# Second expert stage: weighted rows added into the output by the scatters, instead of loads and sums at the end

## What is computed

```python
x = x + 0.5 * _L0_ffn_ref(_layernorm(x, axis=-1), router_w, gate_w, up_w, down_w)
x = x + _L0_attn_ref(_layernorm(x, axis=-1), W_qkv, W_out)
x = x + 0.5 * _L0_ffn_ref(_layernorm(x, axis=-1), router_w, gate_w, up_w, down_w)
```

```python
top_vals, top_idx = jax.lax.top_k(x @ router_w.T, 2)
routing_weights = jax.nn.softmax(top_vals, axis=-1)
combine = jnp.sum(jax.nn.one_hot(top_idx, E) * routing_weights[..., None], axis=1)
for e in range(E):
    y = (jax.nn.silu(x @ gate_w[e].T) * (x @ up_w[e].T)) @ down_w[e].T
    out = out + combine[:, e:e + 1] * y
```

## Time and profile before

| what | us |
| --- | --- |
| median of 3 runs | 1253.74 (1253.63 to 1253.86) |
| profiled execution | 1255.44 |
| its span, first to last instruction | 1253.70 |
| first expert stage, about | 0 to 260 |
| attention, about | 260 to 1016 |
| second expert stage, about | 1016 to 1253.7 |
| first and last start of a scatter in it (line 1250) | 1037.8, 1235.0 |

### The profile page before, as it was taken

The page is one execution under the profiler, slowest core; times in us unless marked ns, Lnnn a source line. Parts: engine busy times, 40 slices in busy tenths (PEclk is TensorE's granted clock), DMA queues, the critical chain, the costliest instruction groups (busy, mean ns, idle before and its releaser), DMA issues. The chain is left out here.

```text
span 1253.7 us, 28419 instructions
## 1 busy us (share of the span) xinstructions
PE 1195.8 (95%) x8838; PEld 911.9 (73%) x8838; DVE 904.5 (72%) x2002; ACT 791.6 (63%) x2272; POOL 810.7 (65%) x884
## 2 busy tenths in 40 slices
PE   7799999979999999999999999999999989999993
PEld 6588888856666666666666667766666668888883
DVE  6775344448888888888888998788998877733543
ACT  4665665646766676667666667766666665555553
POOL 4233356248878778778788787577566536666663
PEclk8899999989999999999999999999999989999997
DMA  9135222132222222222221222221221331113223
GB/s 323 31 97 153 60 55 71 44 72 46 54 60 54 46 56 54 58 46 51 60 57 41 57 60 60 60 52 36 51 52 40 97 116 43 45 48 114 62 65 116
DMA packets 81614, 86.54 MB, mean 69 GB/s; under 512 B 11248, under 2 KB 70512, under 8 KB 81088
## 3 DMA queue, kind: packets, MB, share of 16 engines
q1 hardware_dynamic: 70976, 64.98, 20.0%
q0 software_dynamic: 8864, 18.17, 5.6%
q10 hardware_dynamic: 1632, 1.57, 0.4%
HBM read 33.43 MB, written 17.69 MB: 41 GB/s over the span
## 5 line engine op out<-in xcount | busy, mean ns | idle before, releaser
L2003 POOL TENSOR_SCALAR at_prob<-at_prob,at_rec 128x128 f32<-128x128 f32 (+3 forms) x256 | 312.0, 1223 | 156.8 <-DVE at_rec L2214 154.8
L2401 ACT ACTIVATE at_prob<-at_s,at_nb 128x128 f32<-128x128 f32 (+3 forms) x512 | 264.7, 535 | 16.9 <-DVE at_nb L2206 13.6
L2412 ACT ACTIVATE at_probT<-at_pt 128x128 f32<-128x128 f32 (+3 forms) x256 | 105.2, 437 | 225.6 <-PE at_pt L2110 225.3
L2206 DVE TENSOR_REDUCE at_nb<-at_s 128x2 f32<-128x256 f32 (+3 forms) x256 | 203.2, 815 | 9.4 <-PE at_s L2096 9.4
L1564 DVE TENSOR_TENSOR f_hid<-f_b,f_silu 128x512 f32<-128x512 f32 x142 | 98.4, 693 | 135.8 <-PE f_b L1311 96.1
L2110 PE MATMUL at_pt<-ident,at_prob 128*128 128x128 f32 x1280 | 183.9, 276 | 5.2 <-DVE at_prob L2217 1.9
L2200 DVE TENSOR_TENSOR at_turned<-at_pj,rope 128x1024 f32<-128x1024 f32 x122 | 148.7, 1219 | 46.2 <-PE at_pj L2057 43.2
L2091 PE MATMUL at_s<-at_KT,at_QT 64*128 64x128 f32 (+3 forms) x1024 | 176.5, 463 | 4.9 <-DMA at_KT<-at_probT 2.7
L1997 POOL TENSOR_TENSOR at_R<-at_turned 128x512 f32<-128x512 f32 x126 | 157.5, 1270 | 24.1 <-DVE at_turned L2200 24.1
L2110 PEld LDWEIGHTS at_pt<-ident,at_prob 128*128 128x128 f32 x1280 | 141.7, 142 | 26.7 <-issue 14.6
L2121 PE MATMUL at_o<-at_probT,at_V 128*64 128x128 f32 (+2 forms) x1792 | 152.9, 322 | 0.0
(11 more groups left out here) (336 smaller groups left out, 2258.3 us busy)
## 6 DMA issues: line engine op xcount, KB each, us to landing
at_QT<-at_R SPq DMA_DIRECT2D x128, 128.0 KB, 2.4
at_KT<-at_R SPq DMA_DIRECT2D x124, 128.0 KB, 2.4
ys_dram<-y SPq DMA_DIRECT2D x71, 64.0 KB, 1.8
f_down<-down_t SPq DMA_DIRECT2D x2, 2048.0 KB, 7.6
f_xb<-xn_dram,f_source POOLq DMA_INDIRECT x142, 2.6
X<-x SPq DMA_DIRECT2D x4, 512.0 KB, 6.1
gate<-gate_t SPq DMA_DIRECT2D x8, 256.0 KB, 5.1
f_up<-up_t SPq DMA_DIRECT2D x8, 256.0 KB, 6.7
```

Source lines behind the costliest of these rows:

```text
L2003: pool.tensor_scalar(w, w, rec[:, q, 1:2], None, ALU.mult).then_inc(probB_ready, 1)
L2206: dve.tensor_reduce(nb[:, q, :], s_bank[q % 2][:, :, 0:(q + 1) * P], axis=AX, op=ALU.max, negate=True).then_inc(nb_ready, 1)
L2401: act.activation(prob[q][:, h, :], s_bank[q % 2][:, h, 0:n], ACT.Exp, bias=nb[:, q, h:h + 1], scale=1.0, accum_out=sums[:, q, h:h + 1]).th ...
L2412: act.activation(probT[0][:, 0:q + 1, q * P:(q + 1) * P], pt_bank[0][:, at:at + (q + 1) * P].rearrange("p (b r) -> p b r", r=P), ACT.Copy) ...
```

## The change

The second stage no longer brings rows back. Its scatters add each row straight into `out`, which holds X by then:

- The normed rows of the second stage are stored twice, in `xw_dram`, once for each of a token's two experts, with 129 columns. The 129th is the token's weight for that expert, stored apart by `store_shares` as single numbers, once for the leading half (in attention) and once for the rest (in the second stage).
- A gather brings 129 columns, so each row comes with its weight. There are seven tiles `xb` instead of four (`HELD`), since the weight is read later than the row. DVE multiplies the hidden product by it, in one `scalar_tensor_tensor` in the place of `tensor_tensor`.
- The scatter writes to `out` with `compute_op=ALU.add`. Scatter 0 waits until all of X is stored in `out`, and scatter j waits until scatter j-1 has landed. Rows without a token go to 128 further rows at the end of `out`, which the host cuts off. `targets` takes eight operations for its list in the place of six, `sources` two in the place of four.
- X is stored to `out` during attention, a group at a time (`FINISHED`), the last group at the start of the second stage. The late rows are stored after four blocks have been turned.
- The weights are made earlier: for the leading half in attention, for the rest in steps 6 (`odds`) and 9 (`shares`) of the second stage.
- All loads, sums and stores behind the last scatter and the sums between the steps are gone; the end waits for the last scatters.
- At the beginning of attention PE does 24 transposes whose result nobody reads (`WARM`), ahead of the wait for the first copies of QT and KT.

```diff
     def gather(...):
         if j in (0, sure):
-            pool.wait_ge(self.xn_out, 16 * (self.NB // 4 if j else self.LEAD // 4))
-        rows = self.NB * P if j >= sure else self.LEAD * P
+            pool.wait_ge(self.xn_out, 32 * (self.NB // 4 if j else self.LEAD // 4))
+            pool.wait_ge(self.shares_out, 64 if j else 32)
+        rows = 2 * (self.NB if j >= sure else self.LEAD) * P
         pool.indirect_dma_start(
-            out=self.xb[j % self.AHEAD][:, :], out_offset=None, in_=self.xn_dram[0:rows, :],
+            out=self.xb[j % self.HELD][:, :], out_offset=None, in_=self.xw_dram[0:rows, :],
...
     def store(self, sp, g, xn):
         sp.wait_ge(self.xn_ready, g + 1)
-        sp.dma_start(self.xn_dram[4 * g * P:4 * (g + 1) * P, :].rearrange("(n p) d -> p n d", p=P), xn[:, :, :]
-                     ).then_inc(self.xn_out, 16)
+        for k in range(2):
+            sp.dma_start(self.rows(g, k)[:, :, 0:P], xn).then_inc(self.xn_out, 16)
+
+    def store_shares(self, sp, r):
+        sp.wait_ge(self.shares_ready, r + 1)
+        tiles = self.routing.tiles[r]
+        for k in range(2):
+            sp.dma_start(self.rows(tiles.start // 4, k, len(tiles))[:, :, P:P + 1],
+                         self.routing.wts[:, 2 + k, tiles.start:tiles.stop].rearrange("p (n a) -> p n a", a=1),
+                         allow_slow_non_contiguous=True).then_inc(self.shares_out, 16)
...
     # second stage, SP
+                    g = GROUPS - 1
+                    sp.dma_start(out[4 * g * P:4 * (g + 1) * P, :].rearrange("(n p) d -> p n d", p=P),
+                                 X[:, 4 * g:4 * g + 4, :]).then_inc(stored, 16)
+                    sp.wait_ge(xt_psum, AHEAD)
                     for g in LATE_GROUPS:
                         sp.wait_ge(xn_ready, g + 1)
-                        sp.dma_start(xn_dram[4 * g * P:4 * (g + 1) * P, :].rearrange("(n p) d -> p n d", p=P),
-                                     late_xn[:, 4 * g - LEAD:4 * g + 4 - LEAD, :]).then_inc(xn_out, 16)
-                    scattered(sp)
-                    ...
-                    sp.wait_ge(stored, 16 * GROUPS)
+                        for k in range(2):
+                            sp.dma_start(lead.rows(g, k)[:, :, 0:P], late_xn[:, 4 * g - LEAD:4 * g + 4 - LEAD, :]
+                                         ).then_inc(xn_out, 16)
+                    lead.store_shares(sp, 1)
+                    for k in range(AHEAD):
+                        sp.wait_ge(y_out[k], 16 * ((BLOCKS - k + AHEAD - 1) // AHEAD))
...
     # second stage, POOL: scatter(j)
                     pool.wait_ge(routing.lists_ready, routing.TARGETS[j >= SURE])
                     pool.wait_ge(y_ready, j + 1)
+                    if j == 0:
+                        pool.wait_ge(stored, 16 * (GROUPS + 1))
+                    else:
+                        pool.wait_ge(y_out[(j - 1) % AHEAD], 16 * ((j - 1) // AHEAD) + 16)
                     pool.indirect_dma_start(
-                        out=ys_dram, out_offset=bass.IndirectOffsetOnAxis(ap=routing.target[:, j:j + 1], axis=0),
-                        in_=y[k][:, :], in_offset=None).then_inc(y_out[k], 16)
+                        out=out, out_offset=bass.IndirectOffsetOnAxis(ap=routing.target[:, j:j + 1], axis=0),
+                        in_=y[k][:, :], in_offset=None, compute_op=ALU.add).then_inc(y_out[k], 16)
...
     # second stage, ACT
                 for j in range(-1, BLOCKS + 3):
                     step(act, j, j % AHEAD)
+                    if lead and j == CHOOSE_AT + 2:
+                        routing.odds(act, 1, exp_ready)
...
     # second stage, DVE
-                        dve.tensor_tensor(hid[k][:, :], up_bank[k][:, :], silu[k][:, :],
-                                          ALU.mult).then_inc(hid_ready, 1)
+                        if lead:
+                            dve.scalar_tensor_tensor(out=hid[k][:, :], in0=up_bank[k][:, :],
+                                                     scalar=xb[j % len(xb)][:, P:P + 1], in1=silu[k][:, :],
+                                                     op0=ALU.mult, op1=ALU.mult).then_inc(hid_ready, 1)
...
     # attention, SP
+                sp.dma_start(out[NB * P:(NB + 1) * P, :], ident[:, :]).then_inc(lead.stored, 16)
                 for n in range(ROTATIONS):
...
+                    if n - EARLY in FINISHED:
+                        g = FINISHED[n - EARLY]
+                        sp.wait_ge(y_used, 8 * g + 8)
+                        sp.dma_start(out[4 * g * P:4 * (g + 1) * P, :].rearrange("(n p) d -> p n d", p=P),
+                                     X[:, 4 * g:4 * g + 4, :]).then_inc(lead.stored, 16)
...
+                lead.store_shares(sp, 0)
...
     # attention, PE
+                pe.wait_ge(rope_ready, 2)
+                for _ in range(WARM):
+                    pe.transpose(s_bank[0][:, 0, 0:P], ident[:, :], ident[:, :])
                 for i in range(STEPS + 2):
```

More of the change, by code:

```diff
@@ L413, in shares @@
             last.then_inc(done, 1)
-            dve.wait_ge(done, 1)
     def totals(self, dve, r, totals):
@@ L529, in blocked, with first_number @@
                           ALU.is_equal).then_inc(self.block_ready, 1)
+    def first_number(self, r, k):
+        if self.home is not None:
+            return k * self.NB + self.tiles[r].start
+        return 2 * self.tiles[r].start + k * self.n[r]
     def numbered(self, dve, r, k):
@@ L533, in numbered @@
         some = slice(k * n, (k + 1) * n)
-        first = k * self.NB + self.tiles[r].start
+        first = self.first_number(r, k)
         number = self.const.numbersb[:, first:first + n]
@@ L593, in sources @@
         blank, token, found = self.blank[:, some], self.token[:, some], self.found
+        if self.home is None:
+            link(dve.scalar_tensor_tensor(out=token, in0=found[:, 0, some], scalar=float(P), in1=found[:, 1, some],
+                                          op0=ALU.mult, op1=ALU.add))
+            dve.tensor_scalar(self.source[:, some], token, -1.0, 0.0, ALU.add, ALU.max).then_inc(self.lists_ready, 1)
+            return
         link(dve.tensor_scalar(blank, found[:, 0, some], float(self.NB), None, ALU.is_ge))
@@ L690, in __init__ @@
         self.routing.place_lists(room)
-        self.xb = [room(f"xb{k}", [P, P]) for k in range(self.AHEAD)]
+        self.xb = [room(f"xb{k}", [P, P + 1]) for k in range(self.HELD)]
+        self.exp_ready = sem("exp_ready")
+        self.shares_ready = sem("shares_ready")
+        self.shares_out = sem("shares_out")
         self.xb_in = [sem(f"xb_in{k}") for k in range(self.AHEAD)]
@@ L1277, in _ @@
                         scatter(j - 3)
-                if out is not None:
-                    for m, (g, tiles) in enumerate(((BY_POOL, slice(0, 4)), (SHARED, slice(2, 4)))):
-                        some = X[:, 4 * g + tiles.start:4 * g + tiles.stop, :]
-                        for k in range(2):
-                            pool.wait_ge(weighted, 2 * m + k + 1)
-                            if k:
-                                pool.wait_ge(pool_added, 2 * m + 1)
-                            pool.tensor_tensor(some, lead_got[g % LEAD_GROUPS][:, k, tiles, :], some, ALU.add
-                                               ).then_inc(pool_added, 1)
             @block.tensor
@@ L1555, in step @@
                     route_later(j)
-                    if out is not None and j in SUMMED:
-                        sum_leading(SUMMED[j])
                     if projection is not None and j in PREPARED_AT:
@@ L1606, in route_later @@
                         routing.pack(dve, 1)
[L1607 removed]
+                    if j == TAKE_AT + 5 and lead is None:
                         routing.shares(dve, 0, exp_ready)
[L1610 to L1620 removed]
+                    if j == CHOOSE_AT + 5 and lead:
+                        routing.shares(dve, 1, exp_ready, lead.shares_ready)
                 def prepare_first(m):
@@ L1684, in _ @@
                         trailing(SPLIT[j - 1])
-                if projection is None:
-                    routing.shares(dve, 1, exp_ready, shares_ready)
-                    added = 0
-                    for g, tiles in ((BY_DVE[0], range(0, 4)), (BY_DVE[1], range(0, 4)), (SHARED, range(0, 2))):
-                        dve.wait_ge(got_in[g % LEAD_GROUPS], 64)
-                        for k in range(2):
-                            if k:
-                                dve.wait_ge(dve_added, added)
-                            for t in tiles:
-                                n = 4 * g + t
-                                dve.scalar_tensor_tensor(out=X[:, n, :], in0=lead_got[g % LEAD_GROUPS][:, k, t, :],
-                                                         scalar=wts[:, 2 + k, n:n + 1], in1=X[:, n, :],
-                                                         op0=ALU.mult, op1=ALU.add).then_inc(dve_added, 1)
-                                added += 1
         work.close()
@@ L1905, in attention @@
         EARLY = 3
```

(2 more changed lines are left out.)

128 lines of the change are left out of this document (40 added, 88 removed).

## The result

The changed kernel takes 1346.0 us (median of 4 runs, 1345.08 to 1348.26) where the kernel before takes 1253.7 (1253.63 to 1253.86): 1.0732 times as long, with a 95% interval of 1.0718 to 1.0746. That is 92.3 us more; 38 were forecast. The profiled execution took 1348.26 us, its span 1346.5.

A forecast was written before the change was run, and what follows sets the result against it. PE was taken to bound the second stage. First scatter 1034.9, intervals 248.5, last landing 2.8, end 0.4 and crowding 5 made 1291.6, 37.9 over the 1253.7 span; forecast 1292 us, range 1252 to 1350.

The forecast's parts named there:

- the tail: After the last scatter's landing, 1237.25 to 1253.7 us: loads, sums and stores without a matmul; the change removes these 16.4 us.
- serial loop: Second-stage scatters, each waiting for the previous landing: 2.3 + 0.75 + 0.5 = 3.55 us against PE's 2.83; chance 0.66.
- The other signs that were named: Second stage: scatters 3.3-3.9 us apart, landing after 2.6-3.1; span ending within 1 of last landing; 2.4 GHz behind attention's first gap.
- the four tiles y: In the second stage ACT can't overwrite a tile until its scatter lands; PE's y bank stays full, at the loop's pace.
- d: In each adding scatter, reading, adding and writing back beyond a plain write: 0.5 us taken, between 0 and 2.6.
- Uneven intervals: Crowding beside the first scatters: 4 us for the late rows (0 to 8.4), 1 for the weight columns (0 to 4).
- The first scatter: Second stage's beginning: start at 1037.8 - 2.5 (clock in attention) - 0.4 (list on DVE) = 1034.9 us.
- The end: After the last scatter's landing: 0.4 us to the span's end, as before behind the last store's landing.
- the wait hides: In the second stage POOL works ahead while waiting; with d below 0.2 PE stays the bound: 1237 us, chance 0.11.
- The nearly free addition: In the second stage the loop is real but d is under 0.2: 1251 to 1270 us, chance 0.10.
- the third: Second stage: PE's clock falls, 71 steps take 117 us more, 1409; or d is above 1.2; chance 0.13 together.
- Costed at nothing: Weight in the hidden product, WARM, leading tokens' shares, stores of X and xn, wider gathers, odds at step 6: 0 us.

## Why the prediction was right and wrong

**The bound and what becomes of it: right in the main.** PE set the pace, the tail went, and the scatters became a serial loop longer than PE's step: each starts 0.8 us behind the landing of the one before, PE is idle a fifth of the stretch, and the clock is at 0.99. The other signs that were named didn't come. Scatters are 4.08 us apart and not 3.3 to 3.9, they land after 3.3 us and not 2.6 to 3.1, the span ends 2.8 us behind the last landing and not within 1, and behind attention's first gap the clock is still at 0.50 for 6.8 us. The path from the loop to PE was wrong too. The forecast had ACT wait for the four tiles y and PE's idle time end with ACT's y or with hidden work. The first line tells for what PE waited from 1100 to 1230 us (us, times, longest), the second how long ACT's y waited for the landing of a scatter in the whole stage (us, times):

```profile
PE f_b L1285 <- DMA f_xb<-xw_dram,f_source: 27.6, 29, 2.5
```

```profile
  ACT y L1448: 5.9, 2
```

PE's 27.8 idle us end with the landing of a gather. A gather stands behind the waiting scatter in POOL's order, and that, which the forecast set aside, is what holds PE to the loop's pace. The time is the same either way, since POOL's loop sets it.

**The step that failed: d.** It was set at 0.5 us, with ends of 0 and 2.6, as what reading, adding and writing back costs beyond a write. It measured 1.0, and the loop 4.08 instead of 3.55. The 0.5 were made of two things about data: 0.3 us for reading HBM, from gather against scatter, and 0.2 for a second stream of 64 KB. What landing takes more beyond POOL's own instruction is 1.0 - 0.6 = 0.4 us, so for that part the sum was near in size, though the 0.4 are the time by which the data takes longer, in 128 small packets, and no second stream. What it left out is that the instruction itself grows, from 0.985 to 1.587 us, on the engine that issues it; start to landing was read as a transfer's time, though the first 0.98 us of the 2.3 were POOL's instruction. The step that chose d from rows about reading and bytes is the one that failed: the bytes turned out to cost some 0.2 us of the 1.0. The forecast named 7.1 us for each 0.1 of d; 0.5 more of d make 35 of the 37.2 us of the table, and the rest is 0.03 us a turn, about what the wait takes to pass. By the Trainium skill's 0.8 us (DMA: Bandwidth & Descriptors, Latency and other measured facts) d would have come nearer, and still 0.2 short.

**Uneven intervals: undersized.** 5 us were taken, with ends of 0 and 8.4 for the late rows and 4 for the weight columns; the two measured 6.4 and 2.5, each nearer its upper end. What is left of the 16.05, some 7 us, are intervals 0.4 to 1.3 us over the regular one, behind blocks 7, 12, 22, 27, 35, 37, 42, 47, 52 and 57. Most of these stand out in the other adding kernels of the same chain, in the plain chained one 7 and 52 and some others. The forecast had nothing for them. No run was made for their cause, but nine of these ten hold a transfer of 16 KB in queue q8, which the profile calls "instruction". These lines are of the interval behind block 52 (1265.1 to 1270.5 us), first that queue, then the scatter with its time to landing:

```profile
q8 instruction: 1, 0.02, 1.8%
...
out<-y,f_target POOLq DMA_INDIRECT x1, 4.6
```

From block 7 on, the 12 intervals with such a transfer are 0.55 us over the regular one in the mean, the other 51 by 0.01; three of the 12 are of ordinary length. That these transfers are the cause is likely by that, and not shown.

**The first scatter: 1038.64 instead of 1034.9.** Two gains were added up that are not there together in this profile. Attention did end sooner, though only by 1.6 us (PE's first turn of late rows starts at 1016.46, before at 1018.10) where 2.5 were forecast, and so the list came sooner: the first gather starts at 1021.14 where it started at 1022.94. But the second stage's first turn starts at 1025.81 where it started at 1025.62 in the kernel before. Between lie the late rows' router matmuls on PE. Its clock is 0.50 over the whole of 1015.6 to 1032.7, while in the trace of before it was 0.77 in the mean of 1015 to 1020 and 0.84 from 1020 to 1025; from 1005 to 1015, ahead of this, PE had been busy for 6.8 us in the changed kernel and for 8.2 before. These rows show it in the changed kernel:

```profile
1016.46 1.12 PE L1341 MATMUL f_b<-ident,f_late_xn 128*128 128x128 f32 x4 [1.09 <-ACT f_late_xn L1468]
...
1022.54 3.42 PE L1349 MATMUL f_b<-f_router,f_late_xts 128*128 128x8 f32 x16
1025.81 0.45 PE L1285 MATMUL f_b<-ident,f_xb 128*128 128x128 f32 x1
```

In the kernel before the same 16 matmuls stand so:

```profile
1022.71 1.91 PE L1359 MATMUL f_b<-f_router,f_late_xts 128*128 128x8 f32 x16
```

The 16 matmuls of line 1349 took 1.91 us in the kernel before, the 8 ahead of them 1.03 instead of 1.85: 2.3 us lost. And the low clock lasts longer: at 1031.73 a matmul still takes 0.63 us, where one at 1031.39 took 0.40 in the kernel before; y of block 0 is another 0.6 us later by that. So the first scatter stands 0.8 us behind that of the earlier trace rows, 0.2 of it there at the first turn, where 2.9 less were forecast. That the clock is what ate the gain is read from these rows; no run kept it up to show it. Part of the miss is this profile's own. In the seven other kernels that have the transposes and the late stores in the same place the first scatter starts between 1035.42 and 1037.98, and in the kernel before with the transposes at 1035.04. The 16 matmuls take 3.42 us in each of these too. What differs is attention's end: the first turn of late rows starts between 1013.61 and 1016.15 in the seven, and at 1013.55 with the transposes alone.

**The end: 2.8 us instead of 0.4.** The 0.4 was taken from a store of ACT. Here the last work is POOL's, and the chain ends in a record of POOL's sequencer, a DRAIN of 6.11 us that stands behind the last scatter in program order. The second line gives the lengths of the two DRAINs on POOL in ns (the other one belongs to the first stage):

```profile
1340.17 1.77 POOLq L1188
```

```profile
L1188 POOLq DRAIN  x2: 6112/7227/8342, 238.8 to 1340.2; - x2
```

The last scatter starts at 1340.39 and lands at 1343.7; the DRAIN ends at 1346.3 and the span at 1346.5. The kernel with plain scatters of their own rows, which also ends on POOL, lands at 1239.7 and ends at 1241.7; the two with half the rows end only 1.1 and 1.2 us behind their last landing. In the kernel before the last work was a store of ACT's queue, and POOL had no busy time in the last 4 us.

**The rivals.** That the wait hides (1237 us) fell: 61 of the 71 scatters found POOL idle until the landing. The nearly free addition (1251 to 1270) fell in the plain chained kernel, which with an addition that costs nothing at all takes 1279. Of the third, the clock (1409) fell, with 0.99 in the stage; what came is its other half, a d that with its surroundings carries the time above 1341, at d = 1.0 rather than above 1.2, because the beginning, the uneven intervals and the end add 17 us more.

**Costed at nothing, rightly:** the weight in the hidden product, the 516-byte gathers (0.99 us and 2.5 to landing), the odds in the second stage; with neither chain nor addition the step is PE's 2.83 us again. (Two sums of the forecast are slightly off, and its total rests on neither: the odds' 2 x 1.28 - 1.2 is 1.4 us and not 1.6, and d from 0.2 to 1.2 gives 1270 to 1341 us and not 1268 to 1343.)

## What to carry to other kernels

A loop that waits for its own transfer is priced as landing, plus the time from the wait to the next instruction, plus what the issuing engine itself does in the new form of that instruction; ask the last first, since bytes may cost almost nothing. Before a tail is traded for something in every step, multiply: here 16.4 us at the end stood against 70 times the difference between the loop and the step, which was 0.25 us at the best (a plain chained write, 3.08 against 2.83) and 1.25 with the addition (0.79 with the landing asked first, 3.62 against 2.83). Where several waits stand ahead of one DMA instruction of POOL, put the one that ends last first: it was worth 0.47 us per scatter.

## What the runs showed of the hardware beyond that

- An adding scatter of 128 rows from POOL costs its engine 1.59 us and lands after 3.3; a plain one 0.99 and 2.3. Of the 0.60 us more in the instruction about 0.5 don't fall with rows or bytes. The adding one goes out in 128 packets of 512 bytes, the plain one in 16 of 4096.
- Half as many rows shorten a plain scatter's landing by only 0.1 us (2.25 to 2.13), half the bytes an adding one's by 0.1.
- From the passing of its last wait to its start a scatter takes 0.71 to 0.76 us when that wait stands last of three (0.8 from the landing), and 0.3 us from the landing itself when it stands first.
- A kernel whose last work is a transfer of POOL ended 1.9 to 3.0 us after that transfer had landed, with scatters of half the rows 1.1 to 1.2.
- Two stores of 8 KB in pieces of 4 bytes land after 5.4 us, and the interval of the chained scatters beside them is 2.5 us longer here, and 2.6 to 4.7 in the other chained kernels.
